# Linear attention on one core: three unread two-byte products behind the turning of the keys, in each of eight groups

## What is computed

```
keys = elu(einsum('bsd,hdk->hbsk', x, Wks)) + 1
queries = elu(einsum('bsd,hdk->hbsk', x, Wqs)) + 1
values = einsum('bsd,hde->hbse', x, Wvs)
kv_cum = cumsum(einsum('hbsk,hbsd->hbsdk', keys, values), axis=2)
numerator = einsum('hbsdk,hbsk->hbsd', kv_cum, queries)
denominator = einsum('hbsk,hbsk->hbs', cumsum(keys, axis=2), queries)
out = einsum('hbsd,hde->bse', numerator / (denominator + 1e-9), Wo)
h = h + out
```

## Time and profile before

| what | value |
|---|---|
| median of 3 runs | 1052.0 us (1049.91 to 1062.97) |
| the profiled execution | 1049.9 us, span 1048.0 us |
| mean granted clock of TensorE | 0.925 |
| PE busy in the span | 904.0 us (86%) |
| DVE busy | 649.8 us (62%) |
| ACT busy | 368.5 us (35%) |
| the linear attention stage | 116.5 to about 221.7 us of the span |
| one group of it at the upper clock | 11.68 us |

### The profile page before, as it was taken

How to read it: one execution, slowest core, us unless ns; L and a number is a source line. 1 busy time by engine, 2 the same in 40 slices (tenths; PEclk the granted TensorE clock), 3 DMA queues, 4 the chain that set the end, 5 groups by cost and what they waited for, 6 DMA issues and landing times. The chain is left out here.

```text
span 1048.0 us, 17078 instructions
## 1 busy us (share of the span) xinstructions
PE 904.0 (86%) x6611; PEld 454.4 (43%) x6611; DVE 649.8 (62%) x1734; ACT 368.5 (35%) x645; POOL 223.3 (21%) x291
## 2 busy tenths in 40 slices
PE   1988788979997865997898879999998799979998
PEld 0577566652323334762455333333333344443333
DVE  4977556567675264997467554555653555677665
ACT  0113533234543332223435314444444023443222
POOL 2600022215336031430230320121223402100000
PEclk9998899899999986998998968999999688989999
DMA  9300300000000001000000000000000000000000
GB/s 305 84 1 2 98 2 2 2 2 1 1 1 1 1 1 43 2 2 1 1 1 1 1 1 1 1 1 1 2 1 1 1 1 1 1 2 1 5 6 11
DMA packets 11477, 15.41 MB, mean 15 GB/s; under 512 B 8268, under 2 KB 9324, under 8 KB 10398
## 3 DMA queue, kind: packets, MB, share of 16 engines
q1 hardware_dynamic: 9976, 13.20, 4.2%
q10 hardware_dynamic: 1418, 1.09, 0.4%
HBM read 13.76 MB, written 0.52 MB: 14 GB/s over the span
## 5 line engine op out<-in xcount | busy, mean ns | idle before, releaser
L622 DVE TENSOR_REDUCE mx<-PS 128x2 f32<-128x1024 f32 (+3 forms) x104 | 109.6, 1095 | 103.8 <-PE PS L440 96.9
L582 ACT ACTIVATE arena<-PS 128x1024 f32<-128x1024 f32 (+3 forms) x104 | 91.0, 923 | 130.3 <-PE PS L470 130.3
L1217 DVE TENSOR_TENSOR arena<-arena,PS 128x512 f32<-128x512 f32 (+1 forms) x144 | 97.0, 684 | 45.0 <-ACT arena L1192 40.8
L1121 PE MATMUL PS<-XT,late 64*128 64x512 f32 (+1 forms) x288 | 101.9, 650 | 11.0 <-PEq L2502 6.6
L485 PE MATMUL PS<-arena 128*64 128x512 f32 (+3 forms) x416 | 99.8, 569 | 0.5 <-DVE arena L683 0.4
L465 PE MATMUL PS<-arena 32*128 32x512 f32 (+4 forms) x416 | 78.6, 622 | 9.7 <-ACT arena L559 7.4
L1192 ACT ACTIVATE arena<-PS,f_b_sb 128x512 f32<-128x512 f32 x96 | 61.8, 685 | 63.2 <-PE PS L1121 61.8
L1153 PE MATMUL PS<-arena,late 128*64 128x512 f32 (+1 forms) x288 | 81.6, 617 | 0.9 <-DVE arena L1217 0.7
L440 PE MATMUL PS<-arena 32*128 32x512 f32 (+4 forms) x416 | 72.8, 643 | 5.8 <-DVE arena L615 2.6
L1121 PEld LDWEIGHTS PS<-XT,late 64*128 64x128 f32 (+1 forms) x288 | 28.2, 183 | 62.5 <-ACT arena L1192 41.5
L1192 ACT ACTIVATE arena<-PS 114x512 f32<-114x512 f32 x48 | 27.4, 596 | 67.6 <-PE PS L1123 66.9
(11 more groups left out here) (423 smaller groups left out, 1632.9 us busy)
## 6 DMA issues: line engine op xcount, KB each, us to landing
arena<-in_rel SPq DMA_DIRECT2D x4, 1024.0 KB, 11.8
late<-in_edges SPq DMA_DIRECT2D x2, 1024.0 KB, 11.4
late<-in_w_f_w SPq DMA_DIRECT2D x3, 342.0 KB
arena<-in_adj SPq DMA_DIRECT2D x1, 1024.0 KB, 6.7
late<-in_w_f_w SPq DMA_DIRECT2D x2, 512.0 KB, 3.7
Cc<-in_consts SPq DMA_DIRECT2D x1, 916.0 KB
arena<-in_ids ACTq DMA_DIRECT2D x1, 800.0 KB
late<-in_w_f_w SPq DMA_DIRECT2D x4, 128.0 KB, 3.8
```

The costliest lines, as they stand in the source:

```text
L582: nc.scalar.activation(PT[:, s % 2, p, :, queries(c)], PS[:, a:a + 2, queries(c)], ACT.Exp, scale=scale).then_inc(exp_done.sem, 1)
L622: v.reduce_max(mx[:, g % 2, c, 2 * p:2 * p + 2], PS[:, a:a + 2, keys(c)], axis=AX.X).then_inc(max_done.sem, 1)
L1121: ins = nc.tensor.matmul(PS[0:rows, up_bank(n), :], w1(i)[r], XT2[r, b * S:(b + 1) * S], start=True, stop=True)
L1217: nc.vector.tensor_tensor(HG[0:rows, n % 4, :], ha, PS[0:rows, gate_bank(n), :], ALU.mult).then_inc(gated_done.sem, 1)
```

## The change

The change adds one line to PE's stream: three unread products between `turn(g)` and the outputs of the group before, in each of the eight groups. They go to the second bank of T(g), which `state(g)` overwrites later. The line numbers of the changed kernel are one higher from there on.

```diff
                 for g in range(G):
                     diagonals(g)
                     turn(g)
+                    unread(3, bank(("T", g, 0)) + 1)
                     if g >= 1:
                         outs(g - 1, 0)
                         outs(g - 1, 1)
```

## The result

Over 20 runs of each, the changed kernel has a median of 1061.34 us (1052.11 to 1064.9) and the kernel before 1055.4 us (1047.17 to 1075.34). The ratio is 1.007, with a 95% interval of 1.0046 to 1.0094: slower by 0.7%, which is clear of noise but under 2%. The forecast of 1049.4 us was wrong in size and in sign, and the time lies outside its range of 1044 to 1058. The profiled execution took 1064.22 us.

A forecast was written before the change was run, and what follows sets the result against it. PE's order and clock were taken to bound the kernel, in a loop of 11.68 us per group. Low stretch -3.1, group 0 +0.5, other groups 0 gave -2.6 us; from 1052.0 that is 1049.4, range 1044 to 1058 us.

The forecast's parts named there:

- The three products cost nothing in a steady group: Groups 1 to 6, upper clock: the products fit PE's 0.59 us hole behind the transposes; cost 0, upper bound 1.0 us.
- The low stretch: Mid-stage, 185.0 to 191.8 us, clock at 1.2 GHz: denser PE work would remove it, -3.1 us (bounds -3.1 and 0).
- all of it is passed on: Group 0, lower clock: state products begin 0.50 us late and PE hands the whole delay on, +0.5 us.
- a near thing: Whether the clock falls mid-stage: 157.7 to 161.1 had the same holes and busy time, yet stayed at 1.00.
- rival 1: The clock isn't helped, only the cost is left: +0.5 to 1.8 us, 1052.5 to 1053.8 us; chance 0.25.
- The rule of the Trainium skill on long waits: Low clock comes from long waits between matmuls, so filling the stage's short holes returns nothing: sum +0.5 instead of -2.6.
- the same step from 1052.0 gives 1049.4: Whole program: the sum of -2.6 us applied to the median of the runs, 1052.0 us, gives the forecast.
- moves no wait: PE's list: the change adds 24 products and 24 loads, removes nothing and leaves every wait in place.
- a second way to the same side: Behind the stage: later stages start at another moment and the clock falls at other places; priced within rival 2.
- rival 2: Slower: products outlast the hole wherever the clock is low, 0.67 us per such group; 1054 to 1060 us; chance 0.17.
- a mechanism that played no part: Steady groups at 1.2 GHz: products outlast the hole, 0.67 us each; all six low gives 4.5 us, 1056.5 us.
- the pair: Products outlasting the hole at low clock, together with clock falls elsewhere in later stages: 1054 to 1060 us, chance 0.17.

The follow-up runs named there:

- exit14a: Changed kernel with 14 more unread products ahead of the last group's outputs; median 1052.95 us, ratio to the kernel before 1.002.
- exit2b: Kernel before with 2 more unread products ahead of the last group's outputs; median 1060.72 us, ratio 1.0038.
- early2: Changed kernel without the unread pairs ahead of the last group's within-chunk products and ahead of the very last output products; median 1056.58 us, ratio 1.0005.
- before_third: Kernel before, unchanged, run again for another profile; 1062.14 us.
- g0_only: Changed kernel with the three products in group 0 alone; median 1058.36 us, ratio 1.0046.
- g1to7_exit14: Changed kernel without the three products in group 0, with 14 more unread products ahead of the last group's outputs; median 1059.72 us, ratio 1.0048.

## Why the prediction was wrong

*Right, with their sizes.* The three products cost nothing in a steady group at the upper clock: 11.68 us before and after, and 1.67 us from transposes to outputs. PE's wait for L998 fell from 4.3 to 0.2 us. The low stretch is gone, and the stage is 2.9 us shorter (forecast 2.6).

*Mis-sized.* In group 0 the state products start 0.50 us late, as forecast, but "all of it is passed on" is wrong: 0.22 us reach group 1. And the forecast started from 1052.0, the median of three runs; over 20 runs that kernel's is 1055.4. Of the 11.9 us between 1049.4 and 1061.3, 3.4 are this base (the same figure as the branch below, by chance).

*Right by the wrong weight.* I called the low stretch "a near thing" and feared that the clock wouldn't be helped (rival 1). The low stretch came in all five profiles of kernels with open holes in groups 1 to 7, and in none of the fifteen with filled ones. The rule of the Trainium skill on long waits (the page TensorE: Matmul & The Clock Gate, section "Loop structure matters more than you think"), weighed in the prediction, doesn't cover this kernel: the clock falls behind holes of 0.84 and 0.59 us, and three narrow products in the second prevent it.

*The step that failed* is the last: "the same step from 1052.0 gives 1049.4". It carried the stage's -2.6 us to the program's end, as if what lies behind would take as long as before. No term of the sum stood for it. It took 8.4 us longer: 3.4 us are a branch of PE's stream ahead of L2516 that takes 3.71 us in place of 0.37, and about 5 are the clock at other places (0.7, 3.5 and 0.9 in the pieces above). The branch is in no rival; "moves no wait" was true of the stage alone. The clock's part I had as "a second way to the same side" in rival 2, at a chance of 0.17 shared with a mechanism that played no part, and as something random. It isn't all chance: in the profiles, the first piece and the third are long in each of the eight that leave the stage at the changed kernel's moment. That the time landed near this case's range is partly luck, since the branch gave 3.4 us of it. My price for the pair, 1054 to 1060, was a little low even so.

*Shown:* that the loss lies behind the stage; that 3.4 us of it are one wait, ahead of L2516, which is long in all fifteen profiles with products in groups 1 to 7 and in none of the other five; that moving the stage's end moves the first piece between 108.0 and 110.3 in either direction, by added work (exit14a, exit2b) and by work taken away (early2), which is worth about 0.7 us by L2516. *Only argued:* that the long value of 402 to 642 follows from the stage's end. It came in all eight profiles with the changed kernel's moment, but early2 and before_third had the short first piece and a third of 251. *Open:* why PE's branch is long in the one set of kernels and short in the other; what in PE's work ends the second low stretch after 3.4 us in one case and after 6.8 in the other; and why g0_only and g1to7_exit14 are slower in the median than their profiles suggest.

## What to carry to other kernels

A microsecond saved in one stage isn't a microsecond at the end: here the same instructions behind it took 8.4 us longer, nearly three times the saving. Part of that was the clock, which fell at other places, and part a single branch of the engine that had been given more instructions. Neither shows in busy time by line, so look for both. Cut several profiles of both kernels at the same instructions and compare piece by piece before you believe or reject such an edit; one profile of each would have blamed 4.8 us on a part that the change doesn't touch. Where two pieces differ, check first that a low stretch hasn't only crossed the cut, and that no wait at the same clock has grown.

## What was unexpected of the hardware

- With holes of 0.84 and 0.59 us in each 11.7 us of otherwise dense work, the clock went to half for 6.8 us once in the stage in every profile of the kernel before: right behind the two holes of group 5 in one, of group 3 in two.
- One conditional branch on PE's sequencer took 0.37 us in the five profiles of kernels with at most six more PE instructions and 3.4 to 3.9 us in the fifteen of kernels with 40 or more.
- The executions don't come to the stage at random moments: the time from the first L2034 to the next fall lay within 0.49 to 0.77 us in all three profiles of before, and within 0.06 to 0.29 in all three of the changed kernel. What fixes that moment was not looked into.
- The first piece takes fixed values (108.00 eight times to 0.01 us, 110.3 to 110.4 eight times), and the third 249.6 to 249.9 eleven times. So a profiled execution's time is largely a sum of a few steps. That the spread of all runs is made of them too is likely, but wasn't shown.
